# Three additions for five in a convolution's last sums, and output weights mixed by pairs of rows

## The chip, the cores and the metric

The kernel runs on one core of a Trainium2 chip. The metric is the device time of one execution in microseconds (us), the median of several runs; lower is better. The engines are named as in the profile: PE (TensorE matmul), PEld (its weight loads), DVE (VectorE), ACT (ScalarE), POOL (GpSimd) and SP (SyncE, which here only starts DMAs).

## The reference, cut to what matters

Four layers follow each other, each added to `x` (16 batches of 256 rows by 512 columns, fp32) with a gate. The change touches the first two.

```python
# layer 0, attention-like part: 32 heads of 8, a long convolution per head
kv  = jnp.einsum('bhil,bhjl->bijhl', k_, v_)          # k_ = v_ = ctx, q_ = layernorm(x)
y   = jnp.fft.irfft(kv_f * kernel_f, n=fft_size)[..., :L]
out = y + kv * D[None, None, None, :, None]
out = jnp.einsum('bijhl,bhil->bjhl', out, q_)         # sum over i of 8 products
...
# layer 0, feed-forward part: routing (16 batches x 32 experts) mixes the experts' weights
combined     = jnp.einsum('be,bteh->bth', routing, full_expert_outputs)
w_o_dyn      = jnp.einsum('be,ehd->bhd', routing, o_weights)   # o_weights: 32 x 64 x 512
final_output = jnp.einsum('bth,bhd->btd', combined, w_o_dyn)
```

## The kernel before

The program is a row of stages with a barrier between them. Stage 1 normalises `x` and transposes it into `QT`. Stage 2 is the convolution. Stage 3 adds its result to `x`, computes the routing, mixes the expert weights, and applies them. Then come the second attention and the second feed-forward part, which the change leaves alone.

**Stage 2, the convolution (lines 334 to 497).** It goes over 32 heads `h` and two halves of the batches, so over 64 half-heads. The convolution is a matmul: `toep` holds the head's taps as shifted columns, `kv` holds 36 products of context rows (k and v are the same, so 36 of the 64 pairs suffice). Per half-head PE runs 10 fp32 matmuls of 288 columns (line 436, two records each in the trace) into the PSUM buffer `y[half]`, and stops before it if DVE has not yet finished with that buffer: the wait on `s_tt`, two half-heads back. POOL makes the next head's products (`pairs_of`, lines 157 and 160), in even heads also a low part of the context (`low`, line 383, two SBUF inputs: `ct` minus `kh`), and then `turned` (line 374), which multiplies ACT's copy `ym` of part of `y` with the query columns `qc` into `R`. DVE's function `half_head` does the rest: three small products into `R` (lines 470, 473, 475), the large product in place in `y` (line 478), and then the sum of the eight products per output. They lie as four slots of 8 in `y` and four slots of 8 in `R`. Line 481 adds the last slot of both into `X`, line 482 adds the other three slots of `R` to those of `y` in place, and lines 485, 486 and 487 add the three slots of `y` to `X`, the last of them into `QT`. `chain.link` makes DVE wait for its own last instruction. After it `s_tt` is raised and PE may reuse `y[half]`. DVE's and PE's loops (`Fori`) have two heads per turn, so four half-heads.

**Stage 3, the mixing (lines 595 to 1010).** `o_weights` lie in `WOin`, on 128 partitions (4 groups `hq` of 32 experts) with 16 rows of 512 each. SP loads them with four DMAs (line 610), on one semaphore `s_wo`. PE waits for the routing matrix `RB` (`s_rb`) and for all of `s_wo`, and runs 16 fp32 matmuls with 64 output partitions (line 799), alternating between two PSUM banks. ACT copies each result to `WOS` (line 1004), SP stores it to the DRAM tensor `WO` (`mixed_out_weights`) with 16 DMAs of four rows (line 614), `WOS` having two halves that are reused once their stores have landed (`s_wst`). Behind these matmuls PE mixes the value weights (line 804), then goes through the batches by pairs: `inner` (line 748) and `outer` (line 761), which needs `WO` loaded back (line 622, `wo`).

Of the kernel before, what the change touches and what calls it, by code (L numbers as in the profile page):

```python
# [9 lines left out]
ALU = mybir.AluOpType  # L10
ACT = mybir.ActivationFunctionType
# [60 lines left out]
def _build(nc, a, out, whole):  # L72
# [45 lines left out]
    with ExitStack() as era1:  # L118
# [212 lines left out]
        with ExitStack() as st:  # L331
            qc = [sb(st, f"qc{i}", [P, HALF * CB * B8, 2 * HD0]) for i in range(2)]
            R = [sb(st, f"R{i}", [P, CB * B8, 4 * HD0]) for i in range(2)]
            X = [sb(st, f"X{i}", [P, CB * B8, HD0]) for i in range(2)]
            MID = (D4 - 1) * HD0
# [114 lines left out]
            def _(dve):  # L450
# [5 lines left out]
                def half_head(h, u, half):  # L456
# [47 lines left out]
        with ExitStack() as st:  # L504
# [11 lines left out]
            room = sb(st, "room3", [P, 2 * GR * C])  # L516
            WOS = ap(room, 0, [[GR * C, 2], [C, GR], [1, C]])[0:HQ * B]
            WOin = ap(XN, TH * HELD[0] * ROW, [[C, HR], [1, C]])
# [40 lines left out]
            p_v = [pk[i].rearrange("p (a b) -> p a b", b=64) for i in range(2)]  # L559
            p_o = [pk[2 + i][0:HQ * B, :] for i in range(2)]  # L560
            pc = pk[4:6]
            py = [pk[6:8], pk[0:2], pk[2:4]]

            (s_con, s_in4, s_act, s_e0, s_ot, s_t1, s_x1, s_bn, s_mv, s_t2, s_ev, s_gs, s_rs, s_srm, s_ctr, s_dve, s_pe,
             s_sr, s_rm, s_rb, s_wp, s_wd, s_wp2, s_wa, s_hold, s_wo, s_back, s_pc, s_cb, s_py, s_q, s_ql, s_st, s_part, s_sum) = [
                sem(n + "_3", st) for n in (
                    "s_con", "s_in4", "s_act", "s_e0", "s_ot", "s_t1", "s_x1", "s_bn", "s_mv", "s_t2", "s_ev", "s_gs", "s_rs",
                    "s_srm", "s_ctr", "s_dve", "s_pe", "s_sr", "s_rm", "s_rb", "s_wp", "s_wd", "s_wp2", "s_wa", "s_hold",
                    "s_wo", "s_back", "s_pc", "s_cb", "s_py", "s_q", "s_ql", "s_st", "s_part", "s_sum")]
            s_wst = [sem(f"s_wst3{i}", st) for i in range(2)]  # L570
            s_w = [sem(f"s_w3{i}", st) for i in range(4)]
            s_wv = [sem(f"s_wv3{i}", st) for i in range(HR // GR)]
            block = st.enter_context(nc.Block())
# [23 lines left out]
            def _(sp):  # L597
                sp.dma_start(sim, a["sim"].rearrange("(k p) e -> p k e", p=P)).then_inc(s_in4, 16)
                sp.dma_start(eg, a["eg"].partition_broadcast(B)).then_inc(s_in4, 16)
                for n in range(HR // GR):  # L600
                    for hq in range(HQ):
                        sp.dma_start(WV[hq * E0:(hq + 1) * E0, n * GR:(n + 1) * GR, :],
                                     a["w_v"][:, hq * HR + n * GR:hq * HR + (n + 1) * GR, :]).then_inc(s_wv[n], 16)
                for n, b in enumerate(HELD):
# [3 lines left out]
                sp.wait_ge(s_srm, (TH * HELD[-1] + TH) // 4)  # L608
                for hq in range(HQ):
                    sp.dma_start(WOin[hq * E0:(hq + 1) * E0], a["w_o"][:, hq * HR:(hq + 1) * HR, :]).then_inc(s_wo, 16)  # L610
                for n in range(HR // GR):
                    sp.wait_ge(s_wa, (n + 1) * GR)
                    for hq in range(HQ):
                        sp.dma_start(WO[:, hq * HR + n * GR:hq * HR + (n + 1) * GR, :],
                                     WOS[hq * B:(hq + 1) * B, n % 2]).then_inc(s_wst[n % 2], 16)
                for n in range(2):
                    sp.wait_ge(s_wst[n], 16 * HQ * HR // GR // 2)

# [10 lines left out]
                for s in range(4):  # L629
                    load(s)  # L630
                sp.wait_ge(s_wp2, HR)
                for n, b in enumerate(HELD):
# [78 lines left out]
            def _(pe):  # L711
# [97 lines left out]
                inner(1)  # L809
                pe.wait_ge(s_wa, HR)  # L810
                for s in range(PAIRSB):
# [141 lines left out]
            def _(act):  # L953
# [44 lines left out]
                act.activation(t["e"], t["z"], ACT.Exp, bias=zmax, accum_out=zsum).then_inc(s_act, 1)  # L998
                for r in range(HR):
                    act.wait_ge(s_wp2, r + 1)  # L1000
                    n = r // GR
                    if r % GR == 0 and n >= 2:
                        act.wait_ge(s_wst[n % 2], 16 * HQ * (n // 2))
                    act.activation(WOS[:, n % 2, r % GR, :], p_o[r % 2], ACT.Copy).then_inc(s_wa, 1)

# [70 lines left out]
    s_pad = sem("s_pad_7")  # L1076
    s_x = [sem(f"s_x9{i}") for i in range(3)]
    xs = [ap(XN, i * C, [[1, C]]) for i in range(3)]

    def gather(pool, j):  # L1080
        pool.indirect_dma_start(out=xs[j % 3], out_offset=None, in_=XD,
                                in_offset=bass.IndirectOffsetOnAxis(ap=slots[:, j:j + 1], axis=0)).then_inc(s_x[j % 3], 16)

    with ExitStack() as st:
# [49 lines left out]
        def by_expert(bank):  # L1134
# [179 lines left out]
        def _(pool):  # L1314
# [114 lines left out]
            for j in range(TILES9):  # L1429
                if j + 3 < TILES9:  # L1430
                    after(s_xt, pool, j + 1)
                    gather(pool, j + 3)
                pool.wait_ge(s_ys, j + 1)
                after(s_add9, pool, 16 * j)
                pool.indirect_dma_start(out=out["out"], out_offset=bass.IndirectOffsetOnAxis(ap=slots[:, j:j + 1], axis=0),  # L1435
                                        in_=ys[j % 2], in_offset=None, compute_op=ALU.add).then_inc(s_add9, 16)
            pool.wait_ge(s_add9, 16 * TILES9)

        @block.tensor
        def _(pe):  # L1440
# [178 lines left out]
            def across(j):  # L1619
                pe.wait_ge(s_x[j % 3], 16 * (j // 3) + 16)  # L1620
# [198 lines left out]
        def _(dve):  # L1819
# [246 lines left out]
```

## Time and profile before

| | us |
|---|---|
| runs of the kernel (3) | median 1624.83, 1622.52 to 1631.5 |
| span of the profiled execution, first to last instruction | 1622.8 |
| convolution matmuls, first to last start | 45.9 to 378.6 |
| DVE busy from 100 to 160 (inside the convolution) | 51.66 of 60 |
| PE busy in the same 60 us | 58.99 of 60 |
| POOL busy in the same 60 us | 50.66 of 60 |
| first and last start of the output-weight matmuls (line 799) | 449.7 and 466.3 |
| first start of `inner` (line 748) | 482.4 |

The profile names an engine's work by line and tile, `out<-in`. The busy share of PE in the convolution includes matmuls that overlap each other: one lasts 406 ns in the trace while the next starts much earlier, so a short stop between two of them does not show as idle. A stop is better seen in the starts. The time of a run is that of the whole execution; the profiled execution's span lies 2.0 us under the median of the three runs and inside their range, and no separate time of it was recorded.

### The profile page before, as it was taken

The numbers are of one execution on the slowest core, as the hardware profiler recorded it, in microseconds if no ns is written. First come the engines' busy times: TensorE is split into PE (matmuls) and PEld (weight loads), VectorE is DVE, ScalarE is ACT, GpSimd is POOL, SyncE is SP. The second block draws the span as 40 slices with busy tenths as digits, with TensorE's granted clock in tenths as the row PEclk, the third lists the DMA queues.
The fourth block names the chain that finished last, engine by engine and source line by source line (L and its number), as shares of the span: only waits on it lengthen the run. The fifth ranks groups of instructions, "written<-read, shape, count | busy, mean of one in ns | idle before, by whom it ended". The sixth has DMA issues, their size and how long they took to land.

```text
span 1622.8 us, 28609 instructions
## 1 busy us (share of the span) xinstructions
PE 1524.7 (94%) x8929; PEld 1067.6 (66%) x8929; DVE 1189.2 (73%) x1868; ACT 981.3 (60%) x1529; POOL 1031.2 (64%) x855
## 2 busy tenths in 40 slices
PE   4999999998887999999999999888999999999996
PEld 3677777777554644444444444378999998999985
DVE  7788888888827777777777776275777777777774
ACT  6433333334724478888888877746777766766773
POOL 3788888885307588888888887502555555555553
PEclk8999999999998999999999999999999999999998
DMA  7344444445763967777776872581444444444443
GB/s 256 108 131 134 136 142 142 142 132 131 207 176 110 211 163 188 200 187 187 198 190 185 201 188 68 178 303 29 78 78 78 79 78 79 79 78 73 75 77 52
DMA packets 111131, 224.27 MB, mean 138 GB/s; under 512 B 12992, under 2 KB 12992, under 8 KB 110144
## 3 DMA queue, kind: packets, MB, share of 16 engines
q1 hardware_dynamic: 94560, 185.10, 40.3%
q0 software_dynamic: 15904, 37.23, 13.2%
q8 instruction: 49, 0.80, 0.2%
q10 hardware_dynamic: 576, 0.79, 0.2%
q14 instruction: 42, 0.34, 0.1%
HBM read 146.71 MB, written 75.84 MB: 137 GB/s over the span
## 4 chain that ended last, share of the span: by engine, by line
PE 33%; DMA 24%; issue 4%; DVE 4%; ACT 2%; POOL 1%; SPq 0%; ACTq 0%; POOLq 0%; DVEq 0%
DMA out_rows<-XN,slots 22%; PE pB L1471 10%; PE pO L1481 8%; PE pA L1453 7%; PE pO L1494 4%; PE pO L1645 1%; DMA XN<-normed_rows,slots 1%; PE pA L1633 1%; PE pB L1462 1%; PE pA L1549 1%; POOL out_rows L1435 1%; DVE low L1827 1%; DVE XN L2010 0%; DMA qs<-q_low 0%; DVE XN L1944 0%
## 5 line engine op out<-in xcount | busy, mean ns | idle before, releaser
L1827 DVE TENSOR_REDUCE low<-pA 128x2 f32<-128x1024 f32 x256 | 307.0, 1223 | 109.4 <-PE pA L1453 95.8
L1722 ACT ACTIVATE pt<-pB 128x512 f32<-128x512 f32 x512 | 287.7, 594 | 89.7 <-PE pB L1471 81.1
L1435 POOL DMA_INDIRECT out_rows<-XN,slots x71 | 196.9, 2773 | 217.9 <-DMA out_rows<-XN,slots 170.1
L436 PE MATMUL y<-kv,toep 128*128 128x288 f32 x1280 | 326.0, 411 | 9.0 <-DVEq L63 5.8
L436 PEld LDWEIGHTS y<-kv,toep 128*128 128x128 f32 x1280 | 238.0, 190 | 96.8 <-DVEq L63 34.0
L1633 PEld LDWEIGHTS pA<-XN,fc 128*128 128x128 f32 x2272 | 265.6, 192 | 10.9 <-issue 5.6
L1633 PE MATMUL pA<-XN,fc 128*128 128x128 f32 x2272 | 266.4, 276 | 5.0 <-DVE XN L1990 4.0
L1471 PE MATMUL pB<-qs,ks 98*128 98x512 f32 x512 | 226.9, 446 | 3.3 <-ACT pt L1722 2.4
L1471 PEld LDWEIGHTS pB<-qs,ks 98*128 98x128 f32 x512 | 95.6, 188 | 192.2 <-ACT pt L1722 149.2
L406 ACT ACTIVATE ym<-y 128x384 f32<-128x384 f32 (+1 forms) x128 | 52.6, 411 | 228.9 <-PE y L436 228.9
L1787 ACT ACTIVATE proj_high<-WP 128x2048 fp32r x71 | 135.7, 1912 | 83.6 <-PE pO L1645 83.6
L1453 PE MATMUL pA<-ks,qs 96*128 96x512 f32 x512 | 183.4, 401 | 1.5 <-DMA qs<-q_low 1.4
L1996 DVE TENSOR_TENSOR proj_low<-WP,proj_high 128x2048 fp32r<-128x2048 f32 x71 | 162.7, 2292 | 10.4 <-ACT proj_high L1787 5.2
L1397 POOL TENSOR_TENSOR part_sum<-pt 128x1024 f32<-128x1024 f32 x64 | 152.2, 2378 | 23.3 <-ACT pt L1722 17.5
L1402 POOL TENSOR_TENSOR part_sum<-part_sum,pt 128x1024 f32<-128x1024 f32 x64 | 152.6, 2384 | 6.9 <-POOL part_sum L1397 3.8
L1481 PE MATMUL pO<-pt,vt 128*32 128x512 f32 x1024 | 135.9, 604 | 0.0
L1782 ACT ACTIVATE fc<-WF 128x2048 f32 x71 | 134.4, 1894 | 1.3 <-DVEq L1980 1.3
L374 POOL TENSOR_TENSOR R<-ym,qc 128x384 f32<-128x384 f32 (+1 forms) x128 | 99.3, 797 | 53.9 <-ACT ym L406 52.3
L157 POOL TENSOR_TENSOR kv<-kc 128x1024 f32<-128x1024 f32 x64 | 121.3, 1896 | 5.4 <-PEq L425 3.1
L1645 PE MATMUL pO<-proj_high,hh 128*128 128x512 f32 x284 | 118.6, 417 | 3.2 <-DVE proj_low L1996 3.2
L2001 DVE SCALAR_TENSOR_TENSOR XN<-pA,XN 128x512 f32<-128x512 f32 x71 | 49.1, 691 | 92.6 <-ACT XN L1792 92.6
L1645 PE MATMUL pO<-proj_high,hl 128*128 128x512 f32 x284 | 112.3, 395 | 0.0
(294 smaller groups left out, 2448.4 us busy)
## 6 DMA issues: line engine op xcount, KB each, us to landing
ks<-ctx_high SPq DMA_DIRECT2D x62, 256.0 KB, 4.6
qs<-q_high SPq DMA_DIRECT2D x62, 256.0 KB, 6.1
kc<-in_ctx_conv SPq DMA_DIRECT2D x32, 384.0 KB, 5.5
XN<-in_x SPq DMA_DIRECT2D x16, 512.0 KB, 9.8
toep<-kernel_and_skip SPq DMA_DIRECT2D x32, 256.0 KB, 3.5
ct<-in_ctx SPq DMA_DIRECT2D x16, 512.0 KB, 6.6
ctx_high<-kh SPq DMA_DIRECT2D x16, 512.0 KB, 4.5
ctx_low<-kl SPq DMA_DIRECT2D x16, 512.0 KB, 5.2
```

Of the source, the lines that this page charges most:

```text
L436: m = pe.matmul(y[half].rearrange("p (l n) c -> p l n c", l=CB)[:, l, :, 0:PAIRS], toep[u][:, (l - s) * P:(l - s + 1) * P], kv[u][:, half, ...
L1397: pool.tensor_tensor(part_sum[:, 2 * n:2 * n + 2], pt[0][:, 2 * n:2 * n + 2], pt[1][:, 2 * n:2 * n + 2], ALU.add).then_inc(s_add, 1)
L1402: pool.tensor_tensor(part_sum[:, 2 * n:2 * n + 2], part_sum[:, 2 * n:2 * n + 2], pt[2][:, 2 * n:2 * n + 2], ALU.add).then_inc(s_add, 1)
L1435: pool.indirect_dma_start(out=out["out"], out_offset=bass.IndirectOffsetOnAxis(ap=slots[:, j:j + 1], axis=0), in_=ys[j % 2], in_offset=Non ...
L1453: m = pe.matmul(pA[n % 2][:, half, :], qs[u][0:NS, h, m0:m0 + P].bitcast(F32R), ks[u][0:NS, h, :].bitcast(F32R), start=True, stop=True)
L1471: pe.matmul(bank(u, n), ks[u][0:NS + 2, h, s * P:(s + 1) * P].bitcast(F32R), qs[u][0:NS + 2, h, :].bitcast(F32R), start=True, stop=True).t ...
L1481: m = pe.matmul(pO[u % 2][h * HD1:(h + 1) * HD1, :], vt[u][:, s, h * HD1:(h + 1) * HD1], pt[s][:, h, :], start=(s == 0), stop=(s == CB - 1))
L1633: m = pe.matmul(pH[j % 2][:, b * P:(b + 1) * P], fc[j % 2][:, k * C + b * P:k * C + b * P + P], xc[j % 2][:, k * P:(k + 1) * P], start=(k ...
L1645: m = pe.matmul(pY[j % 2], picks[j % 2][:, rows].bitcast(F32R), proj[:, weights].bitcast(F32R), start=(k == 0 and n == 0), stop=(k == CB - ...
L1722: act.activation(pt[s][:, h, :], bank(u, n), ACT.Exp, scale=SCALE1).then_inc(s_exp, 1)
L1827: dve.tensor_reduce(ap(low[u % 2], t % CB * NH + t // CB, [[NH, 2], [1, 1]]), pA[n % 2], op=ALU.max, axis=AX.X, negate=True).then_inc(s_re ...
L1996: dve.tensor_tensor(wpl.bitcast(F32R), ap(WP, e, [[1, CB * C]]), wph[j % 2], ALU.subtract).then_inc(s_low, 1)
```

## The change

It does two independent things.

In the convolution `X` is gone. One addition takes all four slots of `y` and of `R` (one operand in PSUM, one in SBUF) and writes `R`. The second adds slots 2 and 3 of `R` to slots 0 and 1 of `R`, the third adds slot 1 to slot 0 and writes `QT`; both of these have two inputs in SBUF.

In the mixing, `o_weights` come in four chunks of four rows per partition group, 16 DMAs, each chunk with a semaphore of its own. PE takes two rows at a time, the even row into partitions 0 to 63 of a bank, the odd row into 64 to 127. ACT copies both with one instruction, 8 instead of 16. SP stores them with 32 DMAs instead of 16. Renamed semaphores of the last stage are left out here.

```diff
@@ convolution, DVE @@
-                    q0, r, x = half * n * 2 * HD0, R[half], X[half]
+                    q0, r = half * n * 2 * HD0, R[half]
...
                     dve.wait_ge(s_rp, 4 * h + 2 * half + 2)
-                    chain.inc(dve.tensor_tensor(x, pairs(3 * HD0, [[1, HD0]]), ap(r, 3 * HD0, [[W, n], [1, HD0]]), ALU.add))
-                    chain.inc(dve.tensor_tensor(pairs(0, [[1, 3 * HD0]]), pairs(0, [[1, 3 * HD0]]),
-                                                ap(r, 0, [[W, n], [1, 3 * HD0]]), ALU.add))
-                    chain.wait()
-                    chain.link(dve.tensor_tensor(x, pairs(0, [[1, HD0]]), x, ALU.add))
-                    chain.link(dve.tensor_tensor(x, pairs(HD0, [[1, HD0]]), x, ALU.add))
+                    def slots(start, count):
+                        return ap(r, start * HD0, [[W, n], [1, count * HD0]])
+
+                    chain.link(dve.tensor_tensor(slots(0, 4), pairs(0, [[1, W]]), slots(0, 4), ALU.add))
+                    chain.link(dve.tensor_tensor(slots(0, 2), slots(0, 2), slots(2, 2), ALU.add))
                     chain.inc(dve.tensor_tensor(ap(QT, h * HSTEP + half * HALFSTEP, [[HD0, n], [1, HD0]]),
-                                                pairs(2 * HD0, [[1, HD0]]), x, ALU.add))
+                                                slots(0, 1), slots(1, 1), ALU.add))
@@ mixing, SP @@
-                for hq in range(HQ):
-                    sp.dma_start(WOin[hq * E0:(hq + 1) * E0], a["w_o"][:, hq * HR:(hq + 1) * HR, :]).then_inc(s_wo, 16)
                 for n in range(HR // GR):
-                    sp.wait_ge(s_wa, (n + 1) * GR)
+                    sp.wait_ge(s_wvo[n], 16 * HQ)
                     for hq in range(HQ):
-                        sp.dma_start(WO[:, hq * HR + n * GR:hq * HR + (n + 1) * GR, :],
-                                     WOS[hq * B:(hq + 1) * B, n % 2]).then_inc(s_wst[n % 2], 16)
+                        sp.dma_start(WOin[hq * E0:(hq + 1) * E0, n * GR:(n + 1) * GR],
+                                     a["w_o"][:, hq * HR + n * GR:hq * HR + (n + 1) * GR, :]).then_inc(s_wvo[n], 16)
+                for n in range(HR // GR):
+                    sp.wait_ge(s_wa, (n + 1) * GP)
+                    for w in range(2):
+                        for hq in range(HQ):
+                            lo = hq * HR + n * GR + w
+                            sp.dma_start(WO[:, lo:lo + GR - 1:2, :],
+                                         WOS[(w * HQ + hq) * B:(w * HQ + hq + 1) * B, n % 2]).then_inc(s_wst[n % 2], 16)
@@ mixing, PE @@
-                pe.wait_ge(s_wo, 16 * HQ)
                 pe.wait_ge(s_ev, UNITS)
-                for r in range(HR):
-                    if r >= 2:
-                        pe.wait_ge(s_wa, r - 1)
-                    pe.matmul(p_o[r % 2], RB, WOin[:, r, :], start=True, stop=True).then_inc(s_wp2, 1)
+                for i in range(HRP):
+                    if i % GP == 0:
+                        pe.wait_ge(s_wvo[i // GP], 2 * 16 * HQ)
+                    after(s_wa, pe, i - 1)
+                    for w in range(2):
+                        m = pe.matmul(p_o[i % 2][w], RB, WOin[:, 2 * i + w, :], start=True, stop=True)
+                    m.then_inc(s_wp2, 1)
@@ mixing, ACT @@
-                    act.activation(WOS[:, n % 2, r % GR, :], p_o[r % 2], ACT.Copy).then_inc(s_wa, 1)
+                    act.activation(WOS[:, n % 2, i % GP, :], pk[2 + i % 2], ACT.Copy).then_inc(s_wa, 1)
```

On DVE, one half-head of the convolution (the first of a loop turn) stood so before; `R`, `y`, `X`, `qc` are the tiles named above.

```order
L470 TENSOR_TENSOR R<-y,qc 128x8x3x8 [waits s_ym_2]
L473 TENSOR_TENSOR R<-y,qc 128x32x4
L475 TENSOR_TENSOR R<-y,qc 128x32x4
L478 TENSOR_TENSOR y<-y,qc 128x32x32 [waits s_dve2]
L481 TENSOR_TENSOR X<-y,R 128x256 [waits s_rp_2,s_dve2]
L482 TENSOR_TENSOR y<-y,R 128x32x24
L485 TENSOR_TENSOR X<-y,X 128x256 [waits s_dve2]
L486 TENSOR_TENSOR X<-y,X 128x256 [waits s_dve2]
L487 ISA [waits s_dve2]
L487 TENSOR_TENSOR QT<-y,X 128x256
```

The same half-head on DVE with the change, its lines numbered anew:

```order
L472 TENSOR_TENSOR R<-y,qc 128x8x3x8 [waits s_ym_2]
L475 TENSOR_TENSOR R<-y,qc 128x32x4
L477 TENSOR_TENSOR R<-y,qc 128x32x4
L480 TENSOR_TENSOR y<-y,qc 128x32x32 [waits s_dve2]
L486 TENSOR_TENSOR R<-y,R 128x1024 [waits s_rp_2,s_dve2]
L487 TENSOR_TENSOR R<-R 128x32x16 [waits s_dve2]
L488 ISA [waits s_dve2]
L488 TENSOR_TENSOR QT<-R 128x256
```

The four products stand where they stood; five additions have become three, of 1024, 512 and 256 elements per partition, and the last two read `R` alone.

On SP, the queue from the load of the output weights (`in_w_o`) to the reload of the mixed ones stood so before:

```order
L610 DMA XN<-in_w_o 32x8192 [waits s_srm_3,s_hold_3]
L610 DMA XN<-in_w_o 32x8192 x3
L614 DMA mixed_out_weights<-room 16x2048 [waits s_wa_3]
L614 DMA mixed_out_weights<-room 16x2048 x3
...
L622 DMA room<-mixed_out_weights 128x512 [waits s_wst31,s_wst30]
```

With the change, from the last chunk of the load on:

```order
L615 DMA XN<-in_w_o 32x2048 [waits s_wvo33]
L615 DMA XN<-in_w_o 32x2048 x3
L622 DMA mixed_out_weights<-room 16x2x512 [waits s_wa_3]
L622 DMA mixed_out_weights<-room 16x2x512 x7
...
L630 DMA room<-mixed_out_weights 128x512 [waits s_wst31,s_wst30]
```

Of both kinds of store group there are four, one shown. Each now has eight DMAs of half the size in place of four, and the reload stands behind all 32.

## Rows read from the trace of the kernel before

**Rows 1.** Waits from 60 to 370 us: total us, times, longest us.

```profile
PEld y L436 <- DVEq L63: 33.0, 60, 0.9
```

**Rows 2.** Timeline of three half-heads: start us, us, engine, line, operation, [idle before].

```profile
207.13 4.66 PEld L436 LDWEIGHTS y<-kv,toep 128*128 128x128 f32 x20 [0.42 <-DVEq L63]
207.44 0.36 DVE L470 TENSOR_TENSOR R<-y,qc 128x192 f32<-128x192 f32 x1 [0.46 <-PE y L436]
...
209.39 0.42 DVE L481 TENSOR_TENSOR X<-y,R 128x256 f32<-128x256 f32 x1
...
211.18 0.42 DVE L486 TENSOR_TENSOR X<-y,X 128x256 f32<-128x256 f32 x1
...
211.76 0.42 DVE L487 TENSOR_TENSOR QT<-y,X 128x256 f32 x1
...
212.33 4.66 PEld L436 LDWEIGHTS y<-kv,toep 128*128 128x128 f32 x20 [0.54 <-DVEq L63]
212.53 0.36 DVE L470 TENSOR_TENSOR R<-y,qc 128x192 f32<-128x192 f32 x1 [0.34 <-PE y L436]
...
215.17 1.28 POOL L383 TENSOR_TENSOR kl<-ct,kh 128x512 fp32r<-128x512 f32 x1
...
216.60 1.55 POOL L374 TENSOR_TENSOR R<-ym,qc 128x384 f32<-128x384 f32 x2
...
218.01 0.36 DVE L470 TENSOR_TENSOR R<-y,qc 128x192 f32<-128x192 f32 x1 [0.75 <-PE y L436]
```

**Rows 3.** Line 436: duration ns min/median/max, first and last start.

```profile
L436 PE MATMUL y<-kv,toep x1280: 406/406/510, 45.9 to 378.6; 128*128 128x288 f32 x183
```

**Rows 4.** Timeline of PE in the first two half-heads.

```profile
45.92 9.96 PE L436 MATMUL y<-kv,toep 128*128 128x288 f32 x40 [1.98 <-PEq L426]
```

**Rows 5.** DVE's groups: busy us, mean ns of one.

```profile
L478 DVE TENSOR_TENSOR y<-y,qc 128x1024 f32<-128x1024 f32 x64 | 78.1, 1220 | 0.0
...
L2005 DVE TENSOR_TENSOR hl<-XN,hh 128x512 fp32r<-128x512 f32 x71 | 49.2, 693 | 8.4 <-ACT hh L1797 1.4
```

**Rows 6.** Timeline of DVE, 28 to 34.5 us (stage 1).

```profile
27.58 1.69 DVE L234 SCALAR_TENSOR_TENSOR work_<-mv,rstd_ 128x8 f32<-128x8 f32 x1
29.30 0.38 DVE L236 TENSOR_TENSOR work_<-work_,rstd_ 128x8 f32<-128x8 f32 x1
```

**Rows 7.** Timeline of POOL, 26 to 46 us (stage 1).

```profile
27.35 1.89 POOL L157 TENSOR_TENSOR kv<-kc 128x1024 f32<-128x1024 f32 x1 [2.27 <-PE pq L328]
29.21 0.45 POOL L160 TENSOR_TENSOR kv<-kc 128x128 f32<-128x128 f32 x1
```

**Rows 8.** Line 234: ns min/median/max of its seven instructions.

```profile
L234 DVE SCALAR_TENSOR_TENSOR work_<-mv,rstd_ x7: 160/161/1687, 8.2 to 39.5; 128x4 f32<-128x4 f32 x3, 128x2 f32<-128x2 f32 x2, 128x8 f32<-128x8 f32 x2
```

**Rows 9.** Timeline of the mixing, DVE, PE and SP's queue.

```profile
444.87 0.77 DVE L917 COPY RB<-pk 32x16 f32<-32x16 f32 x4 [0.37 <-PE pk L790]
...
449.74 11.34 PE L799 MATMUL pk<-XN,RB 128*64 128x512 f32 x20 [4.93 <-DMA XN<-in_w_o]
...
466.82 14.51 PE L804 MATMUL pk<-RB,WV 128*128 128x64 f32 x128
482.43 3.67 PE L748 MATMUL pk<-QT,WM 128*64 128x256 f32 x32 [1.10 <-DVE WM L922]
...
456.47 13.01 SPq L614 DMA_DIRECT2D mixed_out_weights<-room  x16
471.81 1.77 SPq L622 DMA_DIRECT2D room<-mixed_out_weights  x4
```

**Rows 10.** Line 614: the stores' issues and their time to landing.

```profile
L614 SPq DMA_DIRECT2D mixed_out_weights<-room x16: 302/460/593, 456.5 to 468.9; - x16
...
DMA to landing us min/median/max: 2.5/2.9/3.6
```

**Rows 11.** Line 610: time to landing of the four loads.

```profile
DMA to landing us min/median/max: 7.5/15.2/21.2
```

**Rows 12.** Windows: PE, PEld, DVE, ACT, POOL busy, PEclk, DMA share, GB/s.

```profile
450.00:452.00 2.00, 2.00 (x3) 0.45 (x2) 0.00 (x0) 0.29 (x1) 0.00 (x0) 0.50 0.00 0
```

More of the change, by code:

```diff
@@ L80, in pb @@
         return ctx.enter_context(nc.psum_tensor(name, shape, dt))[:]
+    s_gathered = [sem(f"s_gathered{i}") for i in range(3)]
+    s_added = sem("s_added")
     KP = nc.dram_tensor("kernel_and_skip", [H0, P - 1 + C], F32).ap()
@@ L333, in _build @@
             R = [sb(st, f"R{i}", [P, CB * B8, 4 * HD0]) for i in range(2)]
-            X = [sb(st, f"X{i}", [P, CB * B8, HD0]) for i in range(2)]
             MID = (D4 - 1) * HD0
@@ L516, in _build @@
             room = sb(st, "room3", [P, 2 * GR * C])
-            WOS = ap(room, 0, [[GR * C, 2], [C, GR], [1, C]])[0:HQ * B]
+            GP = GR // 2
+            HRP = HR // 2
+            WOS = ap(room, 0, [[GP * C, 2], [C, GP], [1, C]])
             WOin = ap(XN, TH * HELD[0] * ROW, [[C, HR], [1, C]])
@@ L559, in _build @@
             p_v = [pk[i].rearrange("p (a b) -> p a b", b=64) for i in range(2)]
-            p_o = [pk[2 + i][0:HQ * B, :] for i in range(2)]
+            p_o = [[pk[2 + i][w * HQ * B:(w + 1) * HQ * B, :] for w in range(2)] for i in range(2)]
             pc = pk[4:6]
@@ L568, in _build @@
                     "s_srm", "s_ctr", "s_dve", "s_pe", "s_sr", "s_rm", "s_rb", "s_wp", "s_wd", "s_wp2", "s_wa", "s_hold",
-                    "s_wo", "s_back", "s_pc", "s_cb", "s_py", "s_q", "s_ql", "s_st", "s_part", "s_sum")]
+                    "s_back", "s_pc", "s_cb", "s_py", "s_q", "s_ql", "s_st", "s_part", "s_sum")]
             s_wst = [sem(f"s_wst3{i}", st) for i in range(2)]
             s_w = [sem(f"s_w3{i}", st) for i in range(4)]
-            s_wv = [sem(f"s_wv3{i}", st) for i in range(HR // GR)]
+            s_wvo = [sem(f"s_wvo3{i}", st) for i in range(HR // GR)]
             block = st.enter_context(nc.Block())
@@ L630, in _ @@
                     load(s)
-                sp.wait_ge(s_wp2, HR)
+                sp.wait_ge(s_wp2, HRP)
                 for n, b in enumerate(HELD):
@@ L809, in _ @@
                 inner(1)
-                pe.wait_ge(s_wa, HR)
+                pe.wait_ge(s_wa, HRP)
                 for s in range(PAIRSB):
@@ L998, in _ @@
                 act.activation(t["e"], t["z"], ACT.Exp, bias=zmax, accum_out=zsum).then_inc(s_act, 1)
[L999 to L1003, printed above, removed]
-                    act.activation(WOS[:, n % 2, r % GR, :], p_o[r % 2], ACT.Copy).then_inc(s_wa, 1)
+                for i in range(HRP):
+                    act.wait_ge(s_wp2, i + 1)
+                    n = i // GP
+                    if i % GP == 0 and n >= 2:
+                        act.wait_ge(s_wst[n % 2], 16 * 2 * HQ * (n // 2))
+                    act.activation(WOS[:, n % 2, i % GP, :], pk[2 + i % 2], ACT.Copy).then_inc(s_wa, 1)
                 def hidden(s):
@@ L1076, in _build @@
     s_pad = sem("s_pad_7")
-    s_x = [sem(f"s_x9{i}") for i in range(3)]
     xs = [ap(XN, i * C, [[1, C]]) for i in range(3)]
@@ L1152, in _build @@
         pY = pO
-        s_xt, s_xc, s_h, s_hr, s_hq, s_low, s_w9, s_y, s_ys, s_add9 = [sem(n + "_9", st) for n in (
-            "s_xt", "s_xc", "s_h", "s_hr", "s_hq", "s_low", "s_w", "s_y", "s_ys", "s_add")]
+        s_xt, s_xc, s_h, s_hr, s_hq, s_low, s_w9, s_y, s_ys = [sem(n + "_9", st) for n in (
+            "s_xt", "s_xc", "s_h", "s_hr", "s_hq", "s_low", "s_w", "s_y", "s_ys")]
         def after(signal, eng, n):
@@ L1433, in _ @@
                 pool.wait_ge(s_ys, j + 1)
-                after(s_add9, pool, 16 * j)
+                after(s_added, pool, 16 * j)
                 pool.indirect_dma_start(out=out["out"], out_offset=bass.IndirectOffsetOnAxis(ap=slots[:, j:j + 1], axis=0),
-                                        in_=ys[j % 2], in_offset=None, compute_op=ALU.add).then_inc(s_add9, 16)
-            pool.wait_ge(s_add9, 16 * TILES9)
+                                        in_=ys[j % 2], in_offset=None, compute_op=ALU.add).then_inc(s_added, 16)
+            pool.wait_ge(s_added, 16 * TILES9)
         @block.tensor
@@ L1619, in across @@
             def across(j):
-                pe.wait_ge(s_x[j % 3], 16 * (j // 3) + 16)
+                pe.wait_ge(s_gathered[j % 3], 16 * (j // 3) + 16)
                 after(s_xc, pe, j - 1)
@@ L2008, in scaled @@
                 dve.wait_ge(s_y, j + 1)
-                after(s_add9, dve, 16 * (j - 1))
+                after(s_added, dve, 16 * (j - 1))
                 dve.tensor_scalar(ys[j % 2], pY[j % 2], share[:, j:j + 1], None, ALU.mult).then_inc(s_ys, 1)
```

10 lines of the change are left out of this document (5 added, 5 removed).

## The prediction

> **What bounds the kernel now.** I read the waits of the convolution first. PE's weight load waits for DVE's queue 60 times in 310 us [rows 1]: nearly every half-head starts with PE waiting for DVE to give its buffer back. The timeline shows the ring. PE starts at 207.13, DVE takes up that half-head at 212.53, 5.40 later, and PE gets DVE's older buffer at 212.33, 0.15 after DVE's last sum ended at 212.18 [rows 2]. DVE's work on one half-head lasts 207.44 to 212.18, 4.74 us. So two half-heads cost 5.40 + 4.74 + 0.15 = 10.29, or 5.15 each. Where DVE's loop turns (every fourth) it starts 0.75 us after its last sum, not 0.35 (218.01 against 217.27) [rows 2], which brings the mean to (378.6 - 45.9) / 64 = 5.20 [rows 3]. PE alone could do one in about 4.9 to 4.95: its first two, with no wait between, took 9.96 with the tail [rows 4]. So DVE's chain is worth cutting, down to PE's floor 0.25 us below, and anything that lengthens it is paid almost in full, 64 times.
>
> Stage 3 comes behind a barrier, so both stages' changes add. There `RB` is ready at 445.64, but the first matmul on the output weights starts at 449.74, held by their load; from there to the value mixing at 466.82 are 17.1 us, in which PE alternates with ACT's copies [rows 9].
>
> **The five additions.** The new ones have 1024, 512 and 256 elements. 1024 with one input in PSUM takes 1.22, 512 with both in SBUF 0.69 [rows 5], 256 takes 0.42 [rows 2]. The first starts 1.95 after DVE's start (209.39 against 207.44); between linked instructions lie 0.03, before the last 0.16 (211.60 to 211.76) [rows 2]. New length: 1.95 + 1.22 + 0.03 + 0.69 + 0.16 + 0.42 = 4.47, 0.27 less than 4.74. If nothing else happened, the ring would give (5.40 + 4.47 + 0.15) / 2 = 5.01, and with the loop's turn some 5.04: 0.16 x 64 = 10.5 us gained.
>
> **What speaks against it.** The old additions had at most one input in SBUF. The new second and third have two, and POOL is busy 84% of the stage. The trace before has one place where such a pair meets. A tiny addition on DVE (line 234, two SBUF inputs, 8 elements) starts at 27.58 and takes 1.69 us where its six sisters take 0.16 [rows 6, 8]; it ends at 29.27, just after POOL's product that ran from 27.35 to 29.24 [rows 7]. The next, line 236, lasts until 29.68, again just past POOL's next, which ended at 29.66 [rows 6, 7]. So DVE waits inside the instruction for POOL's whole instruction, and gets in between two of them. DVE's additions with `y` show nothing of it (lines 481 and 486 last 0.42 beside a busy POOL) [rows 2]. Whether POOL waits likewise for DVE no row shows; both answers are costed.
>
> The Trainium skill (SBUF — State Buffer, "Who interferes with whom") says that a DVE instruction with two SBUF inputs contends with a GpSimd instruction that reads SBUF, that the first to issue keeps the shared interface for its whole length, and that one with a single SBUF input does not contend. The trace agrees with the half of it that it can show, 1.69 against 0.16 us. By the page POOL waits too and the time is that of the forecast below, 1633; the row alone leaves it between that and the case in which only DVE waits, 1623.
>
> **The collisions, placed.** In even heads POOL's `low` runs 215.17 to 216.45. DVE's half-head that began at 212.53 would ask for its second addition at 215.73: it waits 0.72 and ends at about 217.0 (a blocked one has its start-up behind it: 0.69 less 0.14). The third asks at 217.2, but `turned`, due at 216.60 [rows 2] and held by the second, has the next turn for its larger part (about 1.0 of the 1.55) and runs to 218.0. The third ends at 218.3 instead of 217.27: 1.0 late. The next even-head half begins later, so `low` overlaps only the edge of the second addition, but `turned` again goes before the third: about 0.5 late. In odd heads there is no `low`; `turned` is due 4.27 after PE's start (212.33 to 216.60) [rows 2], that is 4.42 after DVE's previous end, and the third addition at 0.35 + 4.05 = 4.40: nearly a tie, decided one way in one half, costing 0.9, and the other way in the other, where 0.27 is gained. Played forward from these durations over 64 half-heads, letting POOL's own start-up before it reads be 0.1 to 0.3, four half-heads take 21.8 to 22.1 us in place of 20.8, mostly 4.95, 6.2, 4.95, 5.7 or 5.7, 5.8, 4.95, 5.7. That is +14 to +20 us for the stage, and I take **+17**. Its bounds: if only DVE waits and POOL never does, DVE's third addition is mostly free and the stage comes to +7; if every near tie is lost, four half-heads take 22.9, +33. Behind DVE's waiting instruction stand only its own next half-head and, through `s_tt`, PE; ACT's copies of `qc` wait for the same signal and have over 2 us to spare.
>
> **The mixing.** (a) The load no longer holds PE: the first of today's four megabytes lands 7.5 us after issue, the last after 21.2 [rows 11], so chunks one and two are there before `RB`, and the last one at about 449.5, before its two passes are due. PE starts at 445.75: 4.0 gained. (b) Two rows go as two column halves at a time. Line 748 does that today: 32 records of 256 columns in 3.67 us, 0.22 per pair of records [rows 9], so 0.43 per pair at 512 columns and 0.9 per two rows with the hand-over. Eight of these are 7.3, not 17.1. (c) But the stores hold it back. The first two copies are done at 448.5; eight store issues at 0.46 to 0.49 take 3.9 and the last lands 2.9 later [rows 10], at 455.3. Only then may ACT write the first half of `WOS` again, and PE's last two passes hang on those copies; the value mixing begins at about 457.8 in place of 466.82. (a) to (c) together: **-9**. Bounds: -12 if the stores don't hold ACT; -6 if PE's short stops bring the slow clock back. Today the granted clock is 0.50 (1.2 GHz) behind the 5 us stop [rows 12]; that stop is gone, but stops of about 1 us come between the passes.
>
> What I cost at nothing: the value mixing and its copies (14.5 + 1.1 us) are unchanged and hide the tail of the stores. The 32nd store lands at about 467, the reload (issued at 471.81 today [rows 9]) at 470, and `outer` needs it at 477. With 7 us of cover gone, it would cost one for one. The return of the held rows follows the reload and moves up with it.
>
> **The sum.** 1622.8 + 17 - 9 = 1630.8 in the profiled execution; the median lies 2.0 above its span: **1633**, 0.5% slower.
>
> **The rivals.**
> - *No contention in practice* (the tiny additions at 27.6 us are another thing, say an effect of their form). Then -10.5 - 9 = -19.5: **1605**. For it speaks only that no large addition with two SBUF inputs meets POOL in this trace; against it, two instructions of different kinds that each end within 0.02 us of POOL's. 0.12.
> - *DVE waits, POOL doesn't.* +7 - 9 = -2: **1623**, no change. POOL's instruction would run through. No row speaks for or against. 0.2.
> - *The losses add up further:* every near tie is lost in the convolution, +33 - 9: **1649**. It decides if POOL's start-up is under 0.05 us or DVE's chain a little longer than I have it. 0.1.
> - *The forecast*, both engines wait: 1633, own range 1624 to 1643. 0.58.
>
> **Numbers.** Runs of this kernel tell about 0.5%, 8 us, from no change. Slower by more than that: half of the forecast's case and the 1649 one, with the weaker gains of the mixing, 0.42. Faster: the 1605 case and a few hundredths of the others, 0.17. Between: 0.41. The range 1611 to 1647 leaves out the 1605 case and about half of the 1649 one.
>
> **What the new profile would show.** The second addition (128x512, `R<-R`) with a spread from 0.69 to some 1.3 us and the third (`QT<-R`) from 0.42 to over 1.0, each long one ending just past a POOL instruction, proves the contention; constant 0.69 and 0.42 prove it absent. `turned` above 1.0 for its larger part shows that POOL waits too. The starts of PE's half-heads should be uneven, with some 4.95 apart. In stage 3 the first output-weight matmul should start 0.1 behind `RB`, ACT's fifth copy should wait for a store, and `inner` should start 28 rather than 37 us behind `RB`. I am wrong if POOL's work shifts into a phase where its reads miss both additions (the ring is loose by 0.4 us per half-head), or if the stores take longer than the value mixing hides.

## The result and the profile after

| | us |
|---|---|
| before, 4 runs | median 1626.71 (1622.52 to 1631.5) |
| changed, 4 runs | median 1646.71 (1641.56 to 1649.49) |
| ratio | 1.0125, 95% interval 1.0102 to 1.0147 |
| span of the profiled execution | 1644.9 (before 1622.8) |

The change makes the kernel slower by 1.25%, 20 us, where the prediction said 0.5%, 1633. The medians are of the undisturbed executions: four others, one of `e7`, one of `e8` and two of the kernel before beside them, took 1753 to 6716 us. Where the 22.1 us between the two profiled spans arise, read from the same points of both traces:

| stretch | before | after | difference |
|---|---|---|---|
| start to the convolution's last sum | 384.0 | 402.6 | +18.6 |
| last sum to `RB` ready | 61.6 | 62.3 | +0.7 |
| `RB` ready to `inner` | 36.8 | 40.0 | +3.2 |
| `inner` to the next stage's first matmul | 39.9 | 41.9 | +2.0 |
| from there to the end | 1100.4 | 1098.1 | -2.3 |

The change does not reach what the last row covers, and the difference in it says nothing: in the fourteen traces of this document that stretch lasts 1096.1 to 1104.3.

**Convolution.** The views are those of [rows 2]. First the timeline of four half-heads, DVE and POOL, then the lines that touch `R` (ns min/median/max).

```profile
202.27 1.27 POOL L385 TENSOR_TENSOR kl<-ct,kh 128x512 fp32r<-128x512 f32 x1
203.15 0.94 DVE L487 TENSOR_TENSOR R<-R 128x512 f32<-128x512 f32 x1
204.23 1.06 DVE L488 TENSOR_TENSOR QT<-R 128x256 f32 x1
205.43 4.66 PEld L438 LDWEIGHTS y<-kv,toep 128*128 128x128 f32 x20 [1.03 <-DVEq L63]
...
209.25 0.69 DVE L487 TENSOR_TENSOR R<-R 128x512 f32<-128x512 f32 x1
210.09 0.99 DVE L488 TENSOR_TENSOR QT<-R 128x256 f32 x1
211.22 4.66 PEld L438 LDWEIGHTS y<-kv,toep 128*128 128x128 f32 x20 [1.12 <-DVEq L63]
...
214.63 0.69 DVE L487 TENSOR_TENSOR R<-R 128x512 f32<-128x512 f32 x1
215.47 0.43 DVE L488 TENSOR_TENSOR QT<-R 128x256 f32 x1
216.04 4.70 PEld L438 LDWEIGHTS y<-kv,toep 128*128 128x128 f32 x20 [0.15 <-DVEq L63]
...
220.53 1.09 DVE L488 TENSOR_TENSOR QT<-R 128x256 f32 x1
221.76 2.24 PEld L438 LDWEIGHTS y<-kv,toep 128*128 128x128 f32 x10 [1.03 <-DVEq L63]
```

```profile
L376 POOL TENSOR_TENSOR R<-ym,qc x128: 583/886/1439, 50.1 to 397.5; 128x384 f32<-128x384 f32 x64, 128x192 f32<-128x192 f32 x64
...
L487 DVE TENSOR_TENSOR R<-R x64: 691/692/1404, 54.3 to 401.3; 128x512 f32<-128x512 f32 x64
L488 DVE TENSOR_TENSOR QT<-R x64: 425/990/1093, 55.8 to 402.2; 128x256 f32 x64
```

PE's weight loads for the four half-heads start 5.79, 4.81 and 5.72 apart. An addition of 256 elements, 0.43 alone, takes 0.99 to 1.09 in three of the four. In the first the second addition asks at 203.15 while POOL's `low` runs to 203.54, and ends at 204.09: blocked until POOL is through, plus the 0.55 that a blocked one still needs. Over the whole stage 16 of the 64 second additions are long, and each ends 0.55 behind `low`; 47 of the third are, and each ends 0.28 behind the larger part of `turned`. These are the 0.69 and the 0.42 less the 0.14 of the prediction. In the kernel before, the last addition, with one input in PSUM, started while `turned` ran in 63 of 64 half-heads and was never held up:

```profile
L487 DVE TENSOR_TENSOR QT<-y,X x64: 423/425/426, 55.5 to 383.6; 128x256 f32 x64
```

POOL pays as well. In the kernel before the larger part of `turned` never took over 1.00 us; now it takes up to 1.44.

**Mixing.** The same points as in [rows 9], PE's timeline, then the windows (PE, PEld, DVE, ACT, POOL busy, PEclk, DMA share, GB/s).

```profile
465.06 5.66 PE L808 MATMUL pk<-XN,RB 128*64 128x512 f32 x24 [0.95 <-DVEq L929]
473.70 2.60 PE L808 MATMUL pk<-XN,RB 128*64 128x512 f32 x8 [2.98 <-ACT room L1014]
476.23 27.57 PE L814 MATMUL pk<-RB,WV 128*128 128x64 f32 x128
504.90 5.66 PE L756 MATMUL pk<-QT,WM 128*64 128x256 f32 x32 [1.10 <-DVE WM L932]
```

```profile
466.00:470.00 4.00, 4.00 (x20) 1.15 (x18) 0.00 (x0) 2.39 (x4) 0.00 (x0) 1.00 0.30 51
470.00:474.00 4.00, 1.02 (x6) 0.23 (x4) 0.00 (x0) 1.05 (x2) 0.00 (x0) 1.00 0.80 140
474.00:476.00 2.00, 2.00 (x8) 0.35 (x4) 0.00 (x0) 0.04 (x1) 0.00 (x0) 0.71 0.79 141
476.00:505.00 29.00, 27.90 (x132) 27.48 (x132) 8.17 (x16) 1.09 (x2) 0.00 (x0) 0.50 0.72 218
505.00:512.00 7.00, 7.00 (x40) 3.71 (x40) 0.35 (x1) 1.07 (x3) 0.00 (x0) 0.72 0.00 0
```

PE starts 0.1 us behind `RB`, six passes take 5.7, then it stops for 2.98 us for ACT, which waits for the stores, as worked out. The value mixing starts 11.3 us behind `RB`, 0.9 earlier than predicted; the stores land in 2.0 us (median), where 2.9 were assumed. But it takes 27.6 us in place of 14.5 [rows 9]: the granted clock stands at 0.50, 1.2 GHz, from 474.8 to 509.0. It falls 1.1 us after PE has taken up work again, not in the stop. PE is busy all through the value mixing, so nothing shows in its busy share; what shows is the PEclk column and the doubled duration.

### The profile page after: what moved, and what is told of

Read it like the earlier page. It is cut to its first block, busy times and chain, and to the rows that moved or that the text cites. A ratio compares the mean times of both kernels' runs of the same rounds, so it can differ in the third digit from the quotient of the medians.

```text
span 1644.9 us, 28504 instructions
## 1 busy us (share of the span) xinstructions
PE 1527.6 (93%) x8929; PEld 1080.5 (66%) x8929; DVE 1208.1 (73%) x1740; ACT 974.0 (59%) x1521; POOL 1045.2 (64%) x855
## 4 chain that ended last, share of the span: by engine, by line
PE 33%; DMA 25%; issue 4%; DVE 3%; ACT 2%; POOL 1%; ACTq 0%; POOLq 0%; DVEq 0%; SPq 0%
DMA out_rows<-XN,slots 24%; PE pB L1480 10%; PE pO L1490 8%; PE pA L1462 7%; PE pO L1503 4%; DMA XN<-normed_rows,slots 1%; PE pB L1471 1%; DVE low L1836 1%; PE pA L1558 1%; POOL out_rows L1444 1%; PE pO L115 1%; PE pO L1654 1%; PE pA L1565 0%; DVE XN L1953 0%; ACT pt L1731 0%
## 5 line engine op out<-in xcount | busy, mean ns | idle before, releaser
L1406 POOL TENSOR_TENSOR part_sum<-pt 128x1024 f32<-128x1024 f32 x64 | 152.2, 2378 | 21.8 <-ACT pt L1731 16.0
L376 POOL TENSOR_TENSOR R<-ym,qc 128x384 f32<-128x384 f32 (+1 forms) x128 | 113.8, 909 | 58.1 <-ACT ym L408 58.0
## 6 DMA issues: line engine op xcount, KB each, us to landing
kc<-in_ctx_conv SPq DMA_DIRECT2D x32, 384.0 KB, 5.4
```

What stands on the lines that cost most here:

```text
L1406: pool.tensor_tensor(part_sum[:, 2 * n:2 * n + 2], pt[0][:, 2 * n:2 * n + 2], pt[1][:, 2 * n:2 * n + 2], ALU.add).then_inc(s_add, 1)
```

## The experiments

All of them alter the kernel before, unless said otherwise, and each is compared with it on its own chip.

**One half of the change at a time.** `e1` has the convolution's part of the diff alone, `e2` the mixing's alone.

> The kernel before with the three additions alone. If the convolution pays by contention (DVE's two additions with both inputs in SBUF against POOL), the stage is 18 to 19 us longer as in the changed kernel, and so is the kernel: 1645, ratio about 1.011. Rival: the additions cost nothing and the loss is all in the mixing: 1616, a ratio of 0.994.

> The kernel before with the mixing change alone. If PE's stop of 3 us behind the sixth pass brings the slow clock (1.2 GHz) over the whole value mixing, from RB ready to inner are 40 us in place of 37, the kernel is slower by 1 to 4 us. Rival: the slow clock in the changed kernel came with the later phase of the whole program and not with this stop; then value mixing takes 14.5 us and the kernel is 9 us faster, 1617.

| | median | ratio, 95% interval | last sum | `RB` to `inner` |
|---|---|---|---|---|
| e1 | 1642.14 | 1.0102, 1.0080 to 1.0124 | 403.9 | 35.1 |
| e2 | 1618.64 | 0.9943, 0.9923 to 0.9962 | 385.7 | 39.8 |

`e1` is slower by 17 us: the convolution's part costs what it costs in the changed kernel, and its rival is out. Its stage is 19.9 us longer, 1.7 come back between `RB` and `inner`, and the kernel stays 3 us under the expected 1645. `e2` gave both of my numbers, in different executions. Five of its seven took 1613.5 to 1619.2, around the 1617 of the rival; two took 1627.9 and 1629.3, which is 2 to 4 us over its kernel before. The profiled one is of the latter, and its value mixing has the slow clock:

```profile
455.36 2.42 PE L810 MATMUL pk<-XN,RB 128*64 128x512 f32 x8 [2.98 <-ACT room L1016]
457.71 27.57 PE L816 MATMUL pk<-RB,WV 128*128 128x64 f32 x128
486.38 5.84 PE L758 MATMUL pk<-QT,WM 128*64 128x256 f32 x32 [1.10 <-DVE WM L934]
```

No trace was kept of the faster five, but the mean granted clock was recorded for every execution: 0.973 and 0.975 in the two long ones, 0.979 to 0.983 in the five. So the slow clock follows in some executions only; that they all have the same stop of 2.98 us is likely, since the program is the same, and not shown.

**The stop taken away, lengthened, and filled.** `e3` is `e2` with four buffers for ACT's copies, which fit in the same room, so that ACT waits for no store:

```diff
-            WOS = ap(room, 0, [[GP * C, 2], [C, GP], [1, C]])
+            WOS = ap(room, 0, [[GP * C, 4], [C, GP], [1, C]])
...
-                    if i % GP == 0 and n >= 2:
-                        act.wait_ge(s_wst[n % 2], 16 * 2 * HQ * (n // 2))
-                    act.activation(WOS[:, n % 2, i % GP, :], pk[2 + i % 2], ACT.Copy).then_inc(s_wa, 1)
+                    act.activation(WOS[:, n, i % GP, :], pk[2 + i % 2], ACT.Copy).then_inc(s_wa, 1)
```

> The mixing change with four buffers for ACT's copies in place of two, so that none waits for a store. PE should not stop between its eight passes (about 7.5 us), the clock should stay at 2.4 GHz, value mixing take 14.5 us, and inner start 23 to 24 us behind RB against 37 before: 13 us faster than before, 1613. Rival: if passes of column halves or the value mixing are slow by themselves, value mixing takes 27 us again and the kernel is no faster than before.

`e8` is `e3` with a stop put back, longer:

```diff
                     after(s_wa, pe, i - 1)
+                    if i == 7:
+                        pe.wait_ge(s_wst[1], 16 * 2 * HQ)
```

> The mixing with four buffers of run e3, and PE made to wait before its last pass until the second group of stores has landed: a stop of about 7 us right ahead of the value mixing. If a stop there brings 1.2 GHz and the value mixing (64 columns per matmul) can't win the clock back, value mixing takes 27 us in every execution: 7 + 13 = 20 us over e3, 1633. Rival: the clock returns during the value mixing as it did within 5 us in the kernel before; then 7 to 10 us over e3, about 1621.

`e9` is `e2` with the stop filled by idle matmuls, ACT's wait left as it is:

```diff
+                    if i == 6:
+                        stir(pe, pk[5], 12)
                     after(s_wa, pe, i - 1)
```

> The mixing change alone as in e2, with 12 idle matmuls of 128 columns put where PE would wait for the stores (before pass seven). Same wait of ACT for the stores, but PE is busy through it. If the stop is what costs the clock, value mixing takes 14.5 us in all executions and the time is that of e2's fast ones, 1614 to 1619, without those at 1628. Rival: column-half passes bring the slow clock by themselves; then some executions stay at 1628.

| | median | ratio, 95% interval | value mixing | `RB` to `inner` |
|---|---|---|---|---|
| e3 | 1612.87 | 0.9918, 0.9896 to 0.9940 | 14.5 | 23.2 |
| e8 | 1632.0 | 1.0046, 1.0029 to 1.0063 | 27.6 | 43.2 |
| e9 | 1616.04 | 0.9949, 0.9929 to 0.9969 | 14.5 | 27.2 |

PE's timeline of `e3`, of `e8`, of `e9`:

```profile
444.89 7.52 PE L810 MATMUL pk<-XN,RB 128*64 128x512 f32 x32 [0.95 <-DVEq L931]
452.35 14.51 PE L816 MATMUL pk<-RB,WV 128*128 128x64 f32 x128
```

```profile
458.28 1.98 PE L812 MATMUL pk<-XN,RB 128*64 128x512 f32 x4 [5.87 <-DMA mixed_out_weights<-room]
460.19 27.57 PE L818 MATMUL pk<-RB,WV 128*128 128x64 f32 x128
```

```profile
452.35 2.94 PE L115 MATMUL pk<-ident 128*128 128x128 f32 x24
456.39 1.94 PE L812 MATMUL pk<-XN,RB 128*64 128x512 f32 x8 [1.10 <-ACT room L1018]
458.25 14.51 PE L818 MATMUL pk<-RB,WV 128*128 128x64 f32 x128
```

`e3` met its expectation (13 us); it also shows that the stores, now 32 behind each other, are covered without the two-buffer wait. In `e8` the stop was 5.87 us, not 7, and its nine executions all took 1629.6 to 1635.6, at a mean granted clock of 0.968 to 0.973: no group near 1621. In `e9` the wait is there, the stop is 1.10, and the value mixing of the traced execution is at full clock; its seven executions spread over 1612.7 to 1623.1, wider than I expected, but none is at 1628, and the mean granted clock is 0.980 to 0.985 in all of them. The three together put the loss on PE's stop ahead of the value mixing, not on the column halves or on the load in chunks.

**Which of the two additions pays.** `e5` leaves two SBUF inputs to the last addition alone, `e6` to the middle step alone (`ys` are slots in `y`, in PSUM, `slots` those in `R`):

```diff
@@ e5 @@
+                    chain.inc(dve.tensor_tensor(ys(0, 2), ys(0, 2), slots(0, 2), ALU.add))
+                    chain.link(dve.tensor_tensor(slots(2, 2), ys(2, 2), slots(2, 2), ALU.add))
+                    chain.link(dve.tensor_tensor(slots(0, 2), ys(0, 2), slots(2, 2), ALU.add))
+                    chain.inc(dve.tensor_tensor(ap(QT, h * HSTEP + half * HALFSTEP, [[HD0, n], [1, HD0]]),
+                                                slots(0, 1), slots(1, 1), ALU.add))
@@ e6 @@
+                    chain.link(dve.tensor_tensor(slots(0, 4), ys(0, 4), slots(0, 4), ALU.add))
+                    chain.inc(dve.tensor_tensor(ys(0, 1), slots(0, 1), slots(2, 1), ALU.add))
+                    chain.link(dve.tensor_tensor(slots(1, 1), slots(1, 1), slots(3, 1), ALU.add))
+                    chain.inc(dve.tensor_tensor(ap(QT, h * HSTEP + half * HALFSTEP, [[HD0, n], [1, HD0]]),
+                                                ys(0, 1), slots(1, 1), ALU.add))
```

> Convolution of before with only the last addition having two SBUF inputs (four additions: 512, 512, 512 with one input in PSUM, then 256). In the changed kernel the third addition lasted over 0.47 us in 47 of 64 cases, at the cost of some 29 us of DVE time, the second in 16 at 5 us. If the third is what pays, this stage is also longer than before although its elements are as many: by 5 to 18 us, kernel 1631 to 1643. Rival: the second one, against POOL's low part, is what pays; then this one is within 3 us of before.

> Counterpart of the run before it: the middle step has two SBUF inputs (two additions of 256), the last has one in PSUM. Its middle step falls where POOL runs its low part in even heads only, and it holds turned back less. If the third addition is what pays, this stage is near that of before, within 5 us; if the second pays, it is 5 to 18 us longer.

`e7` keeps the three additions and takes POOL's reading away from `low`:

```diff
-                    pool.tensor_tensor(kl[:, th].bitcast(F32R), ct[:, th], kh[:, th], ALU.subtract).then_inc(s_kl, 1)
+                    pool.memset(kl[:, th], 0.0).then_inc(s_kl, 1)
```

> The three additions with POOL's low part of the context replaced by a fill with zeros of the same size (the low part of the context is left out of the computation), so POOL's instruction in even heads no longer reads SBUF. The second addition should last 0.69 throughout. If that is half the loss, the stage comes to +8 to +12 us over before; since turned still stands before the third addition it should stay above +5. Rival: a fill blocks DVE just as a subtraction does; then +18 as in the changed kernel less what the shorter instruction gives.

`e4` has no addition with two SBUF inputs at all; the four slots are summed by one reduction:

```diff
+                    chain.link(dve.tensor_tensor(pairs(0, [[1, W]]), pairs(0, [[1, W]]), ap(r, 0, [[W, n], [1, W]]), ALU.add))
+                    chain.inc(dve.tensor_reduce(ap(QT, h * HSTEP + half * HALFSTEP, [[HD0, n], [1, HD0]]),
+                                                pairs(0, [[1, HD0], [HD0, 4]]), op=ALU.add, axis=AX.X))
```

> Before with the last sums as one addition of 1024 elements in PSUM and one reduction over the four slots, read from PSUM (two instructions, none with two SBUF inputs). If contention is the cause, there is none here and DVE's half-head is 0.2 us shorter (1.95 + 1.22 + 0.16 + 1.22 = 4.55 against 4.74): the stage is 6 to 8 us shorter than before, 1618. Rival: it is not the SBUF inputs but the longer, coarser instructions that put DVE out of step with PE; then this is slower than before as well.

| | median | ratio, 95% interval | last sum | to before's 384.0 |
|---|---|---|---|---|
| e5 | 1652.38 | 1.0173, 1.0143 to 1.0204 | 414.1 | +30.1 |
| e6 | 1634.96 | 1.0066, 1.0045 to 1.0088 | 398.6 | +14.6 |
| e7 | 1627.71 | 1.0023, 1.0008 to 1.0038 | 388.7 | +4.7 |
| e4 | 1613.69 | 0.9928, 0.9906 to 0.9950 | 373.0 | -11.0 |

The additions with two SBUF inputs in `e5`, in `e6`, in `e7`, and the two instructions of `e4`:

```profile
L490 DVE TENSOR_TENSOR QT<-R x64: 426/1152/1242, 55.1 to 413.7; 128x256 f32 x64
```

```profile
L488 DVE TENSOR_TENSOR y<-R x64: 432/432/1149, 56.3 to 397.2; 128x256 f32<-128x256 f32 x64
L489 DVE TENSOR_TENSOR R<-R x64: 417/419/1217, 57.4 to 397.6; 128x256 f32<-128x256 f32 x64
L490 DVE TENSOR_TENSOR QT<-y,R x64: 424/425/426, 58.7 to 398.1; 128x256 f32 x64
```

```profile
L485 DVE TENSOR_TENSOR R<-R x64: 691/692/694, 54.1 to 387.4; 128x512 f32<-128x512 f32 x64
L486 DVE TENSOR_TENSOR QT<-R x64: 424/706/1091, 54.9 to 388.2; 128x256 f32 x64
```

```profile
L481 DVE TENSOR_TENSOR y<-y,R x64: 1231/1233/1233, 53.0 to 370.4; 128x1024 f32<-128x1024 f32 x64
L482 DVE TENSOR_REDUCE QT<-y x64: 1223/1224/1226, 54.4 to 371.8; 128x1024 f32 x64
```

Every addition with two SBUF inputs has a long tail but one, the second of `e7`, beside which POOL reads nothing from SBUF; every one with an input in PSUM is constant to 10 ns, and the reduction too. I had expected 5 to 18 us of `e5` and under 5 of `e6` if the third is what pays; both cost more, 30 and 15. So it is not one of the two that pays: either does when it falls beside a POOL instruction that reads SBUF. `e5` costs more than the whole change: in 63 of its 64 half-heads the last addition falls behind `turned`, which adds 43.0 us to the durations of DVE's additions; in the changed kernel it is 33.5 us, for the second and third together. In `e7` the second addition stays at 0.69 and 14 of the 18.6 us go: they hang on `low` (in the changed kernel all 16 long second additions lay behind it), partly by way of the third addition, of which 32 are long in place of 47. The fill takes 0.52 us where the subtraction took 1.28, but a shorter instruction isn't all of it: in 16 of the 64 half-heads the second addition starts 0.17 to 0.18 us (once 0.08, once 0.13) before the fill ends, and it is not held up by that: it lasts 691 to 694 ns in all 64. How much of the 14 us is due to the fill being shorter, and how much to its reading nothing, was not separated. The +4.7 of `e7` is a little under the least that I had given. `e4` gains 11 us where I had said 6 to 8; why it is more was not looked into. It is the control for the rival that coarser instructions put DVE out of step: its two are the coarsest of all.

**The changed kernel with the stop filled, and once more as it is.** `e11` adds the edit of `e9` to the changed kernel.

> The changed kernel with the 12 idle matmuls of e9 where PE waits for the stores. If the slow clock behind PE's stop is the whole of what the prediction missed, value mixing takes 14.5 us and the kernel comes to what was predicted, 1631 to 1635, 0.5% over before. Rival: the convolution and the mixing hinder each other in some other way, and it stays at 1640 or more.

> The changed kernel once more, on the same chip as the run before it, to see in how many executions the slow clock comes. If it is a matter of chance per execution as in e2 (2 of 7), the times fall into two groups about 13 us apart, around 1634 and 1647. If it comes every time here, all are at 1645 to 1649.

| | median | ratio, 95% interval | executions |
|---|---|---|---|
| e11 | 1636.86 | 1.0067, 1.0043 to 1.0091 | 10, from 1632.8 to 1640.9 |
| e12 | 1648.37 | 1.0120, 1.0080 to 1.0161 | 6: one 1634.5, five from 1647.8 to 1650.4 |

Twelve idle matmuls take 11.5 us off the changed kernel. Traced, `e11` has the value mixing at full clock (the first fence), `e12` not:

```profile
473.94 1.94 PE L810 MATMUL pk<-XN,RB 128*64 128x512 f32 x8 [1.02 <-ACT room L1016]
475.81 14.51 PE L816 MATMUL pk<-RB,WV 128*128 128x64 f32 x128
```

```profile
474.91 2.70 PE L808 MATMUL pk<-XN,RB 128*64 128x512 f32 x8 [2.98 <-ACT room L1014]
477.54 27.57 PE L814 MATMUL pk<-RB,WV 128*128 128x64 f32 x128
```

The median of `e11` is 10 us over its own before where 8 were predicted; the upper end of what I had expected, 1635, is 2 us below it. `e12` falls into the two groups, with a mean granted clock of 0.981 in the short execution and 0.969 to 0.973 in the five long ones; in `e11` it is 0.980 to 0.987.

**A faster version.** The reduction of `e4` with the mixing of `e3`:

> The reduction of e4 and the mixing with four buffers of e3 together. The stages lie one behind the other, so the gains add: 11 to 12 and 12 to 13 us, 1602, a ratio of 0.985. Rival: what one gains is given back at a later stage (the second attention's start, its loads); then over 1607.

Median 1600.16 (1599.12 to 1601.8), ratio 0.9840, 0.9821 to 0.9858: 1.6% faster than before, and the two gains (11.8 and 12.6 us) add up.

## Why the prediction was off

**What was right.** DVE's chain and PE form a ring in which every delay of DVE is paid: the loads wait for DVE's queue 54 times, as long as 1.2 us. The new additions meet POOL, as was read from one instruction of 8 elements in stage 1 [rows 6, 8]; `e1`, `e4` and `e7` show it. POOL waits too, up to 1.44 us against 1.00. The Trainium skill (SBUF — State Buffer, "Who interferes with whom") says that whichever of the two asks second is the one that waits, and that a GpSimd instruction which only writes holds up no addition; the traces agree with both (up to 1.44 us for the larger part of `turned`, which in `e5`, where it asks first in 63 of 64 half-heads, stays at 1.00; and 0.69 throughout for the second addition of `e7`). The size was right as well: +17 predicted, +18.6 measured. Four half-heads take 22.0 us where 21.8 to 22.1 were worked out, and of the two patterns given the second came, 5.69, 5.79, 4.81, 5.73 for 5.7, 5.8, 4.95, 5.7. Two numbers beside it were off: the 21.8 to 22.1 make +16 to +21 for the stage, not +14 to +20, and PE's floor lies at or under 4.81, not at 4.95. In the mixing, the start behind `RB` (0.1), the stop for the stores and the start of the value mixing (11.3 behind `RB` against 12.1) came as said. The rivals at 1605 and 1623 are out, and so is that of 1649 as a mechanism: the ties were not what was lost. That 1646.7 still lies inside 1611 to 1647, by 0.3 us, is luck: the upper end was meant for more losses in the convolution.

**The step that failed** is in the mixing, "What I cost at nothing: the value mixing and its copies (14.5 + 1.1 us) are unchanged", and the bound beside it, "-6 if PE's short stops bring the slow clock back". I had seen the risk and priced it by the passes that are left after the stop, since in the kernel before the clock comes back within some 5 us of the first of them (windows as in [rows 12]):

```profile
454.00:456.00 2.00, 2.00 (x5) 0.53 (x4) 0.00 (x0) 0.75 (x3) 0.00 (x0) 0.83 0.00 0
456.00:460.00 4.00, 4.00 (x10) 0.77 (x9) 0.00 (x0) 2.81 (x5) 0.00 (x0) 1.00 0.68 131
```

I did not ask what stands behind. Only two passes do, and then the value mixing, through which the slow clock lasted to its end in all four traces in which it fell ahead of it (the changed kernel, `e2`, `e8`, `e12`). It costs 27.6 - 14.5 = 13.1 us there and 2.0 in the first `inner` (5.66 against 3.67). The stretch that the term (a) to (c) is about, from `RB` to `inner`, measured +3.2 in the profiled execution, where -9 was predicted; with the stop filled (`e11`) it is 27.15 - 36.78 = -9.6.

**Put together:** 18.6 - 9.6 = +9 without the slow clock, near the +8 on record, and 13 to 15 more with it. It came in most executions of the changed kernel: of ten, eight took 1646.6 to 1650.4. The bound for the mixing should have been +6, not -6 (-9, and 15 back), and the chance for slower higher than 0.42.

**Open.** Why a stop of 2.98 us brings the slow clock in 2 of 7 executions of `e2` and in 8 of 10 of the changed kernel was not settled; the stop is equally long in the traces of both, and the two kernels reach it at different times (452 and 471 us); the executions of `e2` and of `e12` were also on different chips. One of the ten took 1641.6, between the groups, with no trace of it. Its mean granted clock, 0.979, is nearer to the 0.981 of the short execution than to the 0.969 to 0.973 of the eight, so it is counted with those without the slow clock, near the upper end of `e11` (1640.9). That mean is a hint and no proof: in the kernel before, where other stretches have the slow clock too, it goes from 0.972 to 0.986. Nor did I try the load in chunks and the column halves apart.

## What to carry to other kernels

Before an addition on DVE is moved from PSUM to SBUF operands, look whether POOL reads SBUF beside it: here a blocked one of 256 elements took up to 1.24 us (`e5`), as long as one of 1024 elements with an input in PSUM. One addition and one reduction over slots in PSUM replaced the five additions without meeting POOL (`e4`, 11 us less in the stage). When a stop on PE is added or moved, ask which work stands right behind it and price that work at half the clock; a few idle matmuls in the stop, or better a buffer more so that there is none, are cheap insurance (27.2 and 23.2 us from `RB` to `inner`, against 39.8 with the stop and the slow clock).

## What was not expected of the hardware

The value mixing kept PE busy without a gap for 27.6 us at a granted clock of 0.50, and the clock came back only at 509.0, in the first `inner` pass behind it, while in the kernel before the output-weight passes had it back within 5 us (449.7 to 454.7). A blocked DVE addition hides its wait in its own duration: the 256 elements last 1.09 us and no wait is listed. The slow clock can also come with a stop of only 1.10 us: in the traces of `e4`, `e5` and `e10` the value mixing ran at full clock, and then, at 470.9, 512.7 and 458.9, the granted clock fell to 0.50 for 3.4 us, so that the first `inner` took 5.3, 5.4 and 5.3 us; with the same stop of 1.10 it stayed at full clock in the kernel before, `e1`, `e3`, `e6`, `e7`, `e9` and `e11`. In `e10` it reads:

```profile
443.46 14.51 PE L811 MATMUL pk<-RB,WV 128*128 128x64 f32 x128
459.07 5.25 PE L753 MATMUL pk<-QT,WM 128*64 128x256 f32 x32 [1.10 <-DVE WM L929]
```

So the 2.0 us in the first `inner` are not due to the slow value mixing alone. And a stop of the same length has the slow clock behind it in some executions and not in others, which makes one kernel's times fall into two groups 13 us apart: one profile of it is not enough.
